# Who issues the broadcast loads of a two-pass sort: SyncE three groups ahead, or ScalarE two groups ahead

## The reference

```
h = x @ Wn.T + bn;  e = edge_attr @ We.T + be
a = leaky_relu(sum((h[src] + e) * attn));  a = softmax of a over the edges of one dst
x = layernorm(x + relu(segment_sum(h[src] * a, dst)))
agg = segment_sum(x[dst], src);  mean = agg / max(count, 1)
x = layernorm(x + x @ W1.T + b1 + mean @ W2.T + b2)
```

## Time and profile before

| what | us |
|---|---|
| three timed runs | 1456.13, 1458.52, 1459.77 |
| their median | 1458.52 |
| span of the profiled execution | 1457.1 |
| DST group loop, first table copy to last | 70.8 to about 165 |
| one-hot rows of SRC | 167 to 206 |
| SRC group loop | 207 to 314 |
| gathers of x rows (GpSimd) | 248.9 to 383 |

### The profile page before, as it was taken

How to read it: one execution, slowest core, us unless ns; L and a number is a source line. 1 busy time by engine, 2 the same in 40 slices (tenths; PEclk the granted TensorE clock), 3 DMA queues, 4 the chain that set the end, 5 groups by cost and what they waited for, 6 DMA issues and landing times.

```text
span 1457.1 us, 26741 instructions
## 1 busy us (share of the span) xinstructions
PE 1242.0 (85%) x7210; PEld 1047.6 (72%) x7210; DVE 1092.5 (75%) x3970; ACT 784.9 (54%) x1768; POOL 750.0 (51%) x731
## 2 busy tenths in 40 slices
PE   4499867960199999679999999999998999999994
PEld 3388756850088888568888888888886888778783
DVE  8888876885555555278888888888898787867761
ACT  5655773630044444347777777777764444444542
POOL 1057762677767777733433103555531555655563
PEclk9899998985599999889999999999999999999997
DMA  6889898989256666556666767898872233223221
GB/s 201 261 199 216 182 288 227 311 264 370 72 80 91 100 94 91 66 178 229 218 217 225 221 222 255 291 300 293 306 244 90 90 99 91 86 88 96 85 79 42
DMA packets 118161, 260.71 MB, mean 179 GB/s; under 512 B 23505, under 2 KB 56872, under 8 KB 118084
## 3 DMA queue, kind: packets, MB, share of 16 engines
q1 hardware_dynamic: 75738, 193.82, 42.4%
q0 software_dynamic: 40128, 64.45, 19.6%
q10 hardware_dynamic: 2218, 1.58, 0.3%
HBM read 182.23 MB, written 130.49 MB: 215 GB/s over the span
## 4 chain that ended last, share of the span: by engine, by line
PE 59%; DMA 9%; POOL 9%; issue 8%; ACT 7%; DVE 6%; ACTq 0%; POOLq 0%; DVEq 0%
PE bank L1246 32%; PE bank L1236 8%; PE bank L1224 5%; PE bank L1291 4%; DMA xin<-z_scratch,idx_src 4%; PE bank L1287 4%; PE bank L1243 4%; POOL out_rows L465 4%; POOL xin L462 3%; ACT aggn L602 3%; DMA X<-in_x,idx_src 2%; DVE X L747 2%; PE bank L1175 2%; DMA yout<-low_digits_scratch 2%; ACT sel L650 1%
## 5 line engine op out<-in xcount | busy, mean ns | idle before, releaser
L1246 PE MATMUL bank<-w1T,xT 128*128 128x256 f32 x1968 | 491.2, 380 | 0.0
L1246 PEld LDWEIGHTS bank<-w1T,xT 128*128 128x128 f32 x1968 | 343.4, 190 | 66.4 <-issue 0.3
L471 POOL DMA_INDIRECT order_scratch<-pay,rank_i x200 | 196.0, 980 | 240.8 <-DVE xin L747 105.9
L564 ACT ACTIVATE yout<-bank,nmr,rstd 128x256 f32<-128x256 f32 x492 | 251.7, 577 | 7.3 <-DVE nmr L750 7.3
L555 ACT COPY xT<-bank 128x512 f32<-128x512 f32 x346 | 203.0, 588 | 37.6 <-PE bank L1236 25.0
L915 DVE BATCH_NORM_STATS2 stats<-xin 128x6 f32<-128x512 f32 x246 | 158.8, 687 | 76.0 <-DMA xin<-z_scratch,idx_src 54.6
L915 DVE BATCH_NORM_STATS2 stats<-bank 128x6 f32<-128x512 f32 x246 | 168.5, 694 | 58.7 <-PE bank L1246 58.1
L663 ACT COPY agg<-bank 128x257 f32<-128x257 f32 (+1 forms) x200 | 74.4, 372 | 223.3 <-PE bank L1291 216.4
L510 POOL DMA_INDIRECT z_scratch<-xin,idx_out x100 | 156.4, 1564 | 53.3 <-ACT xin L676 30.1
L747 DVE TENSOR_SCALAR xin<-xin,stats,rstd 128x256 f32<-128x256 f32 x492 | 172.2, 412 | 1.0
L465 POOL DMA_INDIRECT out_rows<-yout,idx_out x100 | 100.0, 1000 | 140.6 <-DMA xin<-z_scratch,idx_src 71.8
(11 more groups left out here) (187 smaller groups left out, 1858.5 us busy)
## 6 DMA issues: line engine op xcount, KB each, us to landing
z_scratch<-in_x SPq DMA_DIRECT2D x125, 400.0 KB
xin<-z_scratch SPq DMA_DIRECT2D x97, 512.0 KB, 4.9
out_rows<-yout SPq DMA_DIRECT2D x97, 512.0 KB, 3.1
yout<-keys_scratch SPq DMA_DIRECT2D x50, 256.0 KB, 5.0
kB<-sorted_scratch SPq DMA_DIRECT2D x50, 256.0 KB, 3.4
yout<-low_digits_scratch SPq DMA_DIRECT2D x50, 128.0 KB
xin<-in_edge_attr SPq DMA_DIRECT2D x12, 512.0 KB, 5.1
order_scratch<-pay,rank_i POOLq DMA_INDIRECT x200, 4.3
```

The lines of the kernel that those rows point to most:

```text
L471: g.indirect_dma_start(out=order_dram[k], out_offset=bass.IndirectOffsetOnAxis(ap=rank_i[k][:, t:t + 1], axis=0), in_=pay[:, t, :], in_off ...
L564: a.activation(yout[hu][0:rows, j, :], bank_of(j // 2)[0:rows, (j % 2) * D:(j % 2 + 1) * D], ACT.Identity, bias=nmr[0:rows, slot, j:j + 1] ...
L1246: ins = mm(to, buf[:, jj, c, 0:n], w[:, c, :], start=False, stop=i == len(terms) - 1 and c == 1)
```

## The change

ScalarE issues the two broadcasts of group n + 2 at the end of `upper_across` for group n, through a new function `spread_keys`. The first two groups are issued before the first `upper_across` of DST. Their waits are the same as SyncE's were. SyncE keeps the copies of x, with their wait on `s_kbu`.

```
             for k in (DST, SRC):
-                sp.wait_ge(s_keyd[k], 32)
                 for q in range(Q):
                     n = k * Q + q
-                    wait(sp, s_lbT, n - 3)
-                    wait(sp, s_lbA, n - 3)
-                    sp.dma_start(lowB[n % 4], spread(lowrow_dram[k], q)).then_inc(s_lb[n % 4], 16)
                     wait(sp, s_kbu, n - 3)
-                    sp.dma_start(keyB[n % 4], spread(keyrow_dram[k], q)).then_inc(s_kb[n % 4], 16)
                     if k == DST or q >= 4:
                         copy_x(1)
...
+            def spread_keys(n):
+                if n >= 2 * Q:
+                    return
+                k, q = n // Q, n % Q
+                act.wait_ge(s_keyd[k], 32)
+                wait(act, s_lbT, n - 3)
+                wait(act, s_lbA, n - 3)
+                act.dma_start(lowB[n % 4], spread(lowrow_dram[k], q)).then_inc(s_lb[n % 4], 16)
+                wait(act, s_kbu, n - 3)
+                act.dma_start(keyB[n % 4], spread(keyrow_dram[k], q)).then_inc(s_kb[n % 4], 16)
...
                 is_zero(onehotT[n % 2][:, 1, :], gap_low, made).then_inc(s_lbA, 1)
+                spread_keys(n + 2)
...
                 if k == DST:
                     act.wait_ge(s_bias, 1)
                     act.wait_ge(s_zero, 80)
+                    spread_keys(0)
+                    spread_keys(1)
                 upper_across(k, 0)
```

## The result

| | before | after |
|---|---|---|
| median of the timed runs, us | 1459.1 (4 runs, 1456.1 to 1462.0) | 1469.8 (4 runs, 1467.0 to 1472.5) |
| ratio | 1 | 1.0069, 95% interval 1.0047 to 1.0092 |
| span of the profiled execution, us | 1457.1 | 1465.2 |

The changed kernel is slower, by 0.0069 x 1459.1 = 10.1 us (the two medians lie 10.7 us apart). The forecast was 1464.5 us in a range of 1456 to 1476, 6.0 us slower. So the sign and the range were right, and the cost was about 4 us too small. In the changed kernel `gap` is L597, `is_zero` L602, the two issues L620 (low digits) and L622 (keys), the table copy L659, the lookups L1233, the order's load L477 and the gathers L457.

What follows compares the result with a forecast made beforehand. It took the kernel as bound by ScalarE's ring with TensorE (3.85 us per group) and one SRC stall, up to the gathers. -10.7 + 12.4 + 2.3 + 2 = +6.0 us gave span 1463.1, forecast 1464.5 us, range 1456 to 1476.

Steps and rivals of the forecast that it cites:

- DST ring: DST loop's cycle per group: lookups, gap, is_zero, table copy, TensorE's count, lookups again; period 3.85 us, forecast 4.25.
- The stall goes: Start of SRC: low digits of group 29 late behind 36 copies on SyncE's queue; whole 10.7 us credited.
- The pair in the ring: Two issues behind is_zero delay ScalarE's table copy by 0.4 us in 31 groups: +12.4 us (6 to 23).
- The issues on ScalarE: Prediction's step on ScalarE's slot behind is_zero: one issue free, the second makes the copy 0.4 us late.
- The first two groups: Ahead of the DST loop: early broadcasts of groups 0 and 1 delay the edge features, +2.3 us (0 to 2.7).
- Two groups ahead: Shorter lead, two groups instead of three, beside the 36 copies: 0.5 us for each of four groups, +2 us (0 to 8).
- What is late next: VectorE's take-up of the order moves to 242.5; the order lands at 238, so no wait there.
- That the stall stays: Own queue does not help group 29's low digits in SRC: +14.7 us, 1473 us; chance 0.11.
- Rival 4: Each issue takes 0.53 us on ScalarE, 0.75 us late per group: +16.9 us, 1475 us; chance 0.11.
- rival 1: Costs and credit cancel, the pair costing 0.3 us in the ring: -0.4 us, 1458 us; chance 0.28.
- Rival 2: Faster: the order lands earlier, at 231, for VectorE's take-up; up to 6.5 us gained, 1452 us; chance 0.06.

Runs made afterwards that it cites:

- e4: Changed kernel with 12 instead of 36 copies of x under the one-hot rows of SRC, 55 after the sort; one run of 1469.9 us.
- e5: Kernel before (SyncE issues all broadcasts) with 12 instead of 36 copies of x under SRC's one-hot rows, 55 after the sort; 1452.6 us, ratio 0.9965.
- e9: Same edit as e5 on the kernel before, run once more; 1451.6 us, ratio 0.9949.
- e3: Changed kernel with only the low digits issued by ScalarE behind is_zero, the keys back on SyncE; one run of 1461.1 us.
- e2: Changed kernel with the pair of issues moved ahead of gap, where ScalarE waits for the lookups; 1460.9 us, ratio 1.0019.
- e1: Changed kernel with one more wait: groups 0 and 1 are issued only after 80 of 98 feature tiles; one run of 1462.0 us.
- e6: Changed kernel with the edits of e1, e2 and e4 together; 1455.4 us, ratio 0.9977.
- e7: Kernel before with none of the 36 copies under the one-hot rows of SRC, 67 after the sort; 1461.7 us, ratio 1.0021.
- e8: Kernel before with 24 instead of 36 copies under the one-hot rows of SRC, 43 after the sort; 1453.9 us, ratio 0.9961.

## Why the prediction was right or wrong

All at the first gather, where the changed kernel is 11.77 us later than before (246.75 to 258.52 at SRC 8). The runs split this into 2.28 (features) + 11.78 (DST ring) - 10.73 (stall) + 3.71 (ring in SRC, e4 less e5: 37.52 - 33.81) + 4.73 (backlog, after less e4: 42.25 - 37.52) = 11.77. The sum closes by construction, since each term is a difference of two stretches; what the experiments give is the name of each term. Each is read from one execution, so tenths and hundredths show where a number comes from and not how well it is known.

- **The stall goes: -10.7 forecast, -10.73 measured** (before less e5; -10.95 with e9). Reading the stall as two pieces, 9.1 us of wait and 1.6 us of slow TensorE (the kernel before has a mean granted clock of 0.52 in 229.7 to 235.2 us), held; it counts as gone in the changed kernel because the waits that are there are taken in the backlog's term.
- **The pair in the ring: +12.4 forecast, +15.5 measured.** The mechanism was right: a pair behind `is_zero` delays the copy, one issue does not (e3), and the pair in another slot does not delay it at all (e2). The term that was mis-sized is "The issues on ScalarE", with its 0.4 us for each group. That is the floor, 4.24 - 3.85 = 0.39 us, reached when the keys' issue takes 0.44 us. But that issue took 0.5 us or more in 20 of the 45 issues before 300 us, twice over 1.2 us, and the mean period in DST rose by 11.78 / 24 = 0.49 us, and by as much in e1 and e4. I took one row of SyncE as the duration and not the spread of such issues; the earlier trace rows itself had one of 0.53 us. There are also eight periods of SRC ahead of the first gather, not seven. Why the keys' issue varies was not settled: in e2, where it starts at another point of the group, 13 of 50 were that long; in e1 and e4, in the slot of the change, 29 and 28 of 50.
- **The first two groups: +2.3 forecast, +2.28 measured** at the features' wait, which moved to 64.43 (64.5 forecast). It moved gap 1 by the same amount. That the figures agree so well is luck: e4, with the same code up to there, had gap 1 2.4 us later still, so one execution gives 2.3 and another 4.6 us.
- **Two groups ahead: +2 forecast, +4.73 measured** in the changed kernel, 2.8 in e1. The waits themselves came out near the forecast of about 0.5 us for each of four groups: three groups waited, and it cost 2.3 us. The low digits landed after 8.4 us in the middle and 10.3 at most, and with a period of 4.24 us a lead of two groups is 2 x 4.24 - 0.85 = 7.6 us. The rows named the right figure, the 8.4 us of GpSimd's scatters beside the copies. What the step left out is the other 2.15 us: one keys' issue of 1.29 us, and the lookups behind it that took 2.72 us instead of 1.52 at a mean granted clock of 0.57. The bounds, 0 to 8, held it. At the gather the forecast's 6.0 us fell 5.8 short of 11.8; 3.1 of them are the ring's and 2.15 this one long issue's, so nearly all of it is the duration of the keys' issue.
- **What is late next.** The order's take-up was forecast for 242.5 and came at 244.43; there was no wait for it, as forecast. The load set out at 225.99, earlier than the 233 or 234 that the forecast implied.
- **From the gather to the end.** Of 11.8 us at the first gather 9.9 were left at the last, 10.5 at z, 8.1 in the profiled span and 10.1 to 10.7 by the medians. I took the shift of the gather as that of the end, and by the medians this holds within 2 us. But the forecast was 6.0 for a shift of 11.8 at the gather, so that it came within 4 us of the measured total is in part luck: some of the shift was not left at the end.
- **The rivals.** That the stall stays (1473 us) was the nearest in time and wrong in its mechanism. A queue of its own did take the low digits from behind the copies: they landed after 8.4 us against 12.8, and the stop of 10.02 us became three waits of 2.04 us at most. The Trainium skill's rule on turns between queues (DMA: Bandwidth & Descriptors, "Queues, rings and completion order") agrees with that. By the Trainium skill's rule that other issuing engines only save issue time (same page, "Issuing engines are not separate DMA queues") the stall would have stayed, and here the measurement decides: most of it went. What the same section says of the 16 engines, that they stay shared, agrees with the landings of 2.9 us with fewer copies about (e4) against 8.4. Rival 4, 0.75 us for each group, did not come about, nor did rival 1 with its 0.3 us. Rival 2 needed an earlier landing of the order; that came only with fewer copies (e5, load at 218.90), not with the change.

## What to carry to other kernels

In this kernel a DMA issue was free only as long as it ended before the datapath was ready for the next instruction. Put issues ahead of a wait that lasts longer than they do, not behind a short activation, and count the spread of their durations, not one row: even ahead of a wait, issues of 1.2 to 2.8 us cost groups of the loop up to 2 us (e2, e6). When a small transfer is late behind a bulk copy, first ask how many bytes were put ahead of it; moving 24 of the 36 copies cost nothing in the loop and beat both ways of moving the issue. Bulk work that is taken from one place turns up at another: here the copies moved behind the sort made the last gather land about 4 us later, and with 67 of them they became the wait.

## What the runs showed of the hardware

- The same DMA issue differs by its neighbours. On ScalarE, in the changed kernel, the 128 KB broadcast took 0.33 us almost always, the 256 KB one right behind it 0.44 us at least, 0.48 in the middle and 1.29 at most (2.80 in e2). On SyncE it was the other way round: 0.53 us for the low digits right behind a copy's issue and 0.32 for the keys.
- In six of the eleven profiled executions (before, e2, e6, e7, e8, e9) one issue of a broadcast between 82 and 88 us took 2.4 to 3.0 us. On SyncE (before, 2.73 us) the loop kept its period of 3.85 us, on ScalarE (e2, 2.80 us) the group took 5.82. Why it is long was not tested.
- An activation or a copy that stands behind a DMA issue started about 0.1 us after the issue's end (124.68 to 124.78, 128.93 to 129.02).
- A 128 KB broadcast in the SRC loop landed after 2.9 us on ScalarE's queue with few copies about (e4; 4.4 in e6), after 5.8 us on SyncE's queue with the same few copies (e5, 5.7 to 6.0), and after 8.4 us on ScalarE's queue beside the 36 copies (9.7 in e1).
